# A transformer block with a routed feed-forward: turn 0 on a schedule of its own, and the last sequence routed and scattered in two halves

## The reference

```python
x = x + attention(layernorm(x))        # 16 heads of 32, softmax with a triangular mask
x = x + moe(layernorm(x))

def moe(x):                            # all 8192 tokens together
    scores = sigmoid(x @ router_w.T)
    topk_idx, topk_w = route(scores + e_bias)
    pos = rank of each (token, k) among those of its expert, in order of the tokens
    valid = pos < C                    # C = ceil(1.25 * 8192 / 32) = 320
    dest = expert * C + pos            # slots_token, slots_w filled at dest
    Y = (silu(Xp @ W_gate) * (Xp @ W_up)) @ W_down
    return scatter_add(Y * slots_w) + silu(x @ sg.T) * (x @ su.T) @ sd.T
```

## Time and profile before

| | |
|---|---|
| three runs | 2354.3, 2357.84, 2362.52 us; median 2357.84 |
| the profiled execution | 2342.3 us, its span 2340.6 us |
| busy over the span | PE 2171.2 us (93%), ACT 1636.1 (70%), DVE 1508.6 (64%), POOL 1032.8 (44%) |
| turn 0 | 18.2 (first projection) to 87.4 us |
| turn 1 | 87.4 to 182.8 us |
| turn 2; turn 3, like all up to 15 | 115.5 us; 114.1 us |
| turn 17 | 1871.9 (first output group) to 1938.3 (table load) |
| experts | from 1938.3 us to the end |

### The profile page before, as it was taken

How to read it: one execution, slowest core, us unless ns; L and a number is a source line. 1 busy time by engine, 2 the same in 40 slices (tenths; PEclk the granted TensorE clock), 3 DMA queues, 4 the chain that set the end, 5 groups by cost and what they waited for, 6 DMA issues and landing times. The chain is left out here.

```text
span 2340.6 us, 42190 instructions
## 1 busy us (share of the span) xinstructions
PE 2171.2 (93%) x13932; PEld 1139.9 (49%) x13932; DVE 1508.6 (64%) x5014; ACT 1636.1 (70%) x4025; POOL 1032.8 (44%) x1495
## 2 busy tenths in 40 slices
PE   7578999999999999999999999999998887999997
PEld 3234444444444444444444444444444444666664
DVE  4645666666767676666666667676667664767664
ACT  5688686867777878786868777777777524666664
POOL 3233134434344343434344343434342635777785
PEclk9799999999999999999999999999999997999999
DMA  7022222222222222222222222222212125999996
GB/s 235 16 53 61 56 74 58 72 58 78 62 71 65 68 71 63 75 68 65 64 64 64 64 64 64 64 64 64 64 46 82 29 99 166 248 247 248 244 249 130
DMA packets 158362, 222.40 MB, mean 95 GB/s; under 512 B 37824, under 2 KB 91168, under 8 KB 158144
## 3 DMA queue, kind: packets, MB, share of 16 engines
q1 hardware_dynamic: 129472, 177.58, 25.2%
q0 software_dynamic: 28672, 42.12, 8.8%
HBM read 112.65 MB, written 56.46 MB: 72 GB/s over the span
## 5 line engine op out<-in xcount | busy, mean ns | idle before, releaser
L745 ACT ACTIVATE junk<-junk,nmax 128x512 f32<-128x512 f32 (+3 forms) x1024 | 574.1, 570 | 160.1 <-DVE nmax L1046 157.9
L1046 DVE CUSTOM_DVE_ANT_0 junk<-scores,maskrow 128x512 f32<-128x512 f32 (+3 forms) x1024 | 464.9, 486 | 214.0 <-PE scores L591 185.8
L735 ACT ACTIVATE probs<-scores_T 128x512 f32<-128x512 f32 x640 | 376.4, 605 | 45.4 <-PE scores_T L608 45.3
L1211 POOL TENSOR_SCALAR_AFFINE_SELECT probs<-probs 128x256 f32<-128x256 f32 x512 | 194.5, 416 | 340.0 <-ACT probs L735 339.6
L1219 POOL DMA_INDIRECT slots_dram<-rec,idx x256 | 262.8, 1026 | 116.3 <-issue 80.7
L591 PE MATMUL scores<-stack_k,stack_q 96*128 96x512 f16 (+3 forms) x1024 | 249.0, 304 | 47.5 <-DVE nmax L1046 47.4
L608 PE MATMUL scores_T<-stack_q,stack_k 97*128 97x512 f16 (+3 forms) x1024 | 246.9, 303 | 31.4 <-ACT probs L735 27.5
L1204 POOL TENSOR_TENSOR split_q<-glu,split_q 128x512 f16<-128x512 f32 x64 | 76.9, 1202 | 390.6 <-ACT split_q L685 390.6
L745 ACT ACTIVATION_READ_ACCUMULATOR junk<-junk,nmax 128x1 f32 x1024 | 212.5, 207 | 0.0
L213 PE MATMUL dense<-xT_hi,wqkv_hi 128*128 128x512 f16 x512 | 197.0, 385 | 1.5 <-DVE xT_lo L1017 1.5
L214 PE MATMUL dense<-xT_lo,wqkv_hi 128*128 128x512 f16 x512 | 196.2, 383 | 0.0
(11 more groups left out here) (284 smaller groups left out, 5451.3 us busy)
## 6 DMA issues: line engine op xcount, KB each, us to landing
stack_q<-split_q SPq DMA_DIRECT2D x384, 64.0 KB, 2.0
stack_k<-split_k SPq DMA_DIRECT2D x384, 64.0 KB, 2.1
out<-xres SPq DMA_DIRECT2D x67, 256.0 KB, 3.1
x2n<-in_x SPq DMA_DIRECT2D x64, 256.0 KB, 3.7
xres<-in_x SPq DMA_DIRECT2D x64, 256.0 KB, 3.0
x2n_dram<-x2n SPq DMA_DIRECT2D x16, 1024.0 KB, 4.3
stack_q<-in_W_gate SPq DMA_DIRECT2D x16, 512.0 KB, 3.7
stack_q<-in_W_up SPq DMA_DIRECT2D x16, 512.0 KB, 5.3
```

The source lines that it names most:

```text
L735: act.activation(to, at, ACT.Exp, scale=SCALE / (QS * QS)).then_inc(exp_done, 1)
L745: last = act.activation(x, x, ACT.Exp, scale=-1.0, bias=c["nmax"][:, hg % 2, m:m + 1], accum_out=c["sums"][:, hg % 2, m:m + 1])
L1046: last = dve.tensor_tensor_reduce(out=c["junk"][:, JUNK_AT[f], at:at + cols], in0=ps["scores"][f % 2][:, at:at + cols], in1=c["maskrow"][: ...
L1211: last = pool.affine_select(out=blk, in_=blk, compare_op=ALU.is_ge, fill=0.0, base=0, pattern=[[0, 2], [1, P]], channel_multiplier=-1)
```

## The change

Turn 0 gets a plan of its own (`PLAN_0`): all ten score fills of group 0 (slots 50 to 68) and of group 1 (70 to 88) lie in turn 0, statistics at 42 to 54, and the side steps at earlier slots. ACT issues the k transfers of the first half. For sequence 0, ACT makes no `sums`; TensorE adds the probabilities with a product by ones after `values` (`probability_sums`), and `divide` on DVE takes the place of `spread_inverses`, `den_copy` and `normalise`. In turn 17 the router, the routing steps, `pos`, the places and the scatters are done for tiles 0 and 1, then for tiles 2 and 3, with five routing steps and four place steps a slot. `carried` gets a second copy. The function bodies of routing only get a range of tiles. In the middle turns the slots stay as they were.

```diff
+GROUPS_0 = ([(w, m, 4) for m in range(HG) for w in ("q", "k")] + [("v", t, 4) for t in range(TT)] + [("none", 0, 8)]
+            + [g for t in range(TT) for g in (("xT", t, 1), ("none", 0, 2))])
...
-GROUPS_17 = ([("out", t, 4) for t in range(TT)] + [("none", 0, 4)] + [("x2T", t, 1) for t in range(TT)] + [("router", 0, 4)]
-             + [(w, j, 4) for j in range(2) for w in ("gate", "up")] + [("pos", 1, 1)]
+GROUPS_17 = ([("out", t, 4) for t in range(TT)] + [("none", 0, 4)]
+             + [g for half in range(2) for g in (("x2T", 2 * half, 1), ("x2T", 2 * half + 1, 1), ("router", half, 2))]
+             + [g for half in range(2) for g in (("gate", half, 4), ("up", half, 4), ("pos", 1 + half, 1))]
              + [(w, j, 4) for j in range(2, IB) for w in ("gate", "up")] + [("down", t, 4) for t in range(TT)])
...
+S_AT_0 = {(0, 0): tuple(zip(range(50, 70, 2), range(FILLS))), (0, 1): tuple(zip(range(70, 90, 2), range(FILLS)))}
+S_AT_1 = {at: slots for at, slots in S_AT.items() if at != (1, 1)}
...
-PLAN_17 = Plan(GROUPS_17, 0, 3, ROUTE_STEPS, (), {})
+PLAN_0 = Plan(GROUPS_0, 100, 1, 0, (), {}, S_AT_0, (42, 46, 50, 54))
+PLAN_1 = Plan(GROUPS_1, 126, 1, 0, (), {}, S_AT_1)
+PLAN_17 = Plan(GROUPS_17, 0, 5, ROUTE_STEPS, (), {})
...
+def tiles_of(s):
+
+    if isinstance(s, int) and s >= BATCH - 1:
+        return range(2 * (s - BATCH + 1), 2 * (s - BATCH + 1) + 2)
+    return range(TT)
...
-SPLIT_SLOT = {slot: place for place, slot in zip(range(3, 8), (12, 22, 32, 42, 66))}
-
-BV_SPREAD, BV_PRODUCT, BV_ADDED = 70, 80, 84
-ROW_SLOT = {100 + 4 * hg: hg for hg in range(HG)}
+SPLIT_SLOT = {slot: place for place, slot in zip(range(3, 8), (8, 15, 22, 29, 92))}
+
+BV_SPREAD, BV_PRODUCT, BV_ADDED = 38, 49, 53
+ROW_SLOT = {slot: hg for hg, slot in enumerate((4, 12, 32, 35))}
+
+KEYS_SLOT = 41
...
             def stacks(i):
                 stack_ready(i, 0)
-                for name in ("q", "k"):
+                for name in ("q",) if in_first(i) else ("q", "k"):
                     for n in range(3):
-                        stack(name, n, 0)
+                        stack(sp, name, n, 0)
...
+            def first_keys():
+                act.wait_ge(qk_split, 2 * SHG)
+                for n in range(3):
+                    stack(act, "k", n, 0)
...
+            def probability_sums(s, hg):
+
+                pe.wait_ge(exp_done, (s * HG + hg + 1) * FILLS)
+                columns(ps["scores_T"][1], lambda kt, h: c["ones"][:, 0:HD]).then_inc(den_done, 1)
...
                     if attn and slot in PV_SLOT:
                         values(i - 1, 1 - par, PV_SLOT[slot])
+                        if in_first(i - 1):
+                            probability_sums(i - 1, PV_SLOT[slot])
...
+                if f == 0 and 0 < s * HG + hg <= HG:
+
+                    act.wait_ge(den_done, s * HG + hg)
...
+                        if of and not in_first(of[0]):
                             sums(*of, f)
...
+            def divide(s, hg):
+
+                n = s * HG + hg
+                by_block = c["denT"][:, :].rearrange("p (n r) -> p n r", r=HD)
+                dve.wait_ge(den_done, n + 1)
+                dve.transpose(c["denT"][:, :], ps["scores_T"][1][:, :]).then_inc(den_read, 1)
+                dve.wait_ge(den_read, n + 1)
+                link(dve.reciprocal(c["rden"][:, hg, :], by_block[:, :, 0]))
+                link(dve.tensor_copy(by_block, c["rden"][:, hg, :].unsqueeze(2).broadcast_to([P, SEQ // HD, HD])))
+                need(dve, aT_ready, n)
+                link(dve.transpose(c["att"][:, :], c["denT"][:, :]))
+                dve.wait_ge(o_done, n + 1)
+                dve.scalar_tensor_tensor(c["att"][:, :], ps["o"][:, :], AS, c["att"][:, :], ALU.mult, ALU.mult).then_inc(att_done, 1)
...
-                    if fin and slot >= plan.route_from:
-                        step = (slot - plan.route_from) * plan.route_pace
-                        for route in ROUTE[step:min(step + plan.route_pace, plan.route_now)]:
-                            route(i)
+                    for half, first in plan.route_from.items():
+                        if fin and slot >= first:
+                            step = (slot - first) * plan.route_pace
+                            for route in ROUTE[step:min(step + plan.route_pace, plan.route_now)]:
+                                route(i - 2 + half)
...
-                        if 0 <= step < len(DESTINATIONS):
-                            DESTINATIONS[step](s, bank)
+
+                        pace = 1 if attn else 4
+                        for destination in DESTINATIONS[max(step * pace, 0):max((step + 1) * pace, 0)]:
+                            destination(s, bank)
...
-            for n in range(TT * TOPK):
-                scatter(BATCH - 1, n)
+            for half in range(2):
+                for n in range(2 * TOPK):
+                    scatter(BATCH - 1 + half, n)
```

More of the change, by code:

```diff
@@ L99, in __init__ @@
         self.qlo = {ends[w, g] + 2: (w, g) for g in range(HG) for w in PROJ[0:2] if (w, g) in ends}
[L101 removed]
+        self.route_from = {half: ends.get(("router", half), 0) + 1 for half in range(2) if not half or ("router", half) in ends}
+        self.route_now, self.route_late = route_now, route_late
         self.last_h = ends.get(("up", IB - 1), 0) + 1
[L103 removed]
+        self.dest_from = {n: ends["pos", n] for n in range(3) if ("pos", n) in ends}
         self.scatter = {slot: (m, n) for m, slots in scatters.items() for n, slot in enumerate(slots)}
[L108 to L115 removed]
+        self.scores = {slot: (back, hg, f) for (back, hg), slots in (scores or S_AT).items() for slot, f in slots}
+        self.maxima = {slot + 1: at for slot, at in self.scores.items()}
+        self.maxima_T = {slot + 2: (back, hg) for slot, (back, hg, f) in self.scores.items() if f == FILLS - 1}
+        self.sums = {slot + 1: at for slot, at in self.maxima.items()}
+        self.shift = {slot + 2: at for slot, at in self.maxima_T.items()}
+        self.inverses = {slot + 5: at for slot, at in self.maxima_T.items()}
+        self.stat1 = {slot: t for t, slot in enumerate(stats)}
+        self.scale1 = {slot + 2: t for t, slot in enumerate(stats)}
+        self.ln1 = {slot + 10 - t: t for t, slot in enumerate(stats)}
 QUARTER = (0, 30, 60, 90)
@@ L388, in in_first, with score_group, stack @@
             return isinstance(i, int) and i == 0
-        def score_group(i, hg, proj, attn, f=FILLS):
-            if hg == 0 or (hg == 1 and f < S_EARLY):
-                return (i, hg) if proj else None
-            return (i - 1, hg) if attn else None
+        def score_group(i, back, hg, proj, attn):
+            if back:
+                return (i - 1, hg) if attn else None
+            return (i, hg) if proj else None
+        def stack(eng, name, n, half):
+            groups, part = slice(half * SHG, (half + 1) * SHG), {"q": (0, 1, 0), "k": (0, 0, 1)}[name][n]
+            for h in range(GH):
+                eng.dma_start(c["stack_" + name][n * HD:(n + 1) * HD, groups, h, :],
+                              c["split_" + name][part][h * HD:(h + 1) * HD, groups, :]).then_inc(stacked[half], 16)
         @block.sync
@@ L766, in turn @@
                         exp(i - 1, *EXP_SLOT[slot])
-                    if attn and slot in READ_SLOT:
+                    if attn and slot in READ_SLOT and not in_first(i - 1):
                         den_copy(i - 1, READ_SLOT[slot])
@@ L771, in turn @@
                     copies(par, slot, groups)
-                    if nxt and slot in LN1_SLOT:
-                        norm1(i + 1, LN1_SLOT[slot])
+                    if in_first(i) and slot == KEYS_SLOT:
+                        first_keys()
+                    if nxt and slot in plan.ln1:
+                        norm1(i + 1, plan.ln1[slot])
                     if fin and slot in plan.ln2:
@@ L965, in dest_equal @@
                 taken()
-                for t in range(TT):
+                for t in tiles_of(s):
                     last = dve.tensor_tensor(c["eq"][:, t, :, :], c["sc"][:, t, :].unsqueeze(1).broadcast_to([P, TOPK, E]),
@@ L1176, in _ @@
             chain["turn"] = chain["links"]
-            turns(dve, counted)
+            turns(dve, turn)
             for n, (name, _) in enumerate(WEIGHTS):
```

282 lines of the change are left out of this document (140 added, 142 removed).

## The result

The changed kernel takes **2349.24 us** in the median of 13 runs (2345.31 to 2353.09), the kernel before, run beside it, 2359.42 in 13 runs (2354.3 to 2362.52). The ratio is 0.9957, with an interval of 0.9949 to 0.9966: 10.2 us less, or 0.43%, with the whole interval outside the 0.3% that the prediction took as the least that can be told. The prediction had 2347.0 and a difference of 10.8.

What follows compares the result with a forecast made beforehand. VectorE was taken to bound turn 0's score half, ScalarE to lead two quarters of turn 1, a chain turn 17's end. 2342.3 - 8.6 - 2.2 + 0 = 2331.5, with 15.5 carried over 2347.0 us; range 2335 to 2358.

Steps and rivals of the forecast that it cites:

- Turn 0: Beginning of the kernel: earlier first score and less VectorE work in the score half start turn 1 8.6 us earlier.
- The issues: Turn 0: ScalarE issues 12 k transfers at 0.635 us each, bringing the first score at 56.0 instead of 57.75.
- the bound for a slow issue: Turn 0: at 1.28 us an issue, first score at 63.7 and turn 1 only 1.4 us earlier.
- Turn 1, new: Turn 1: sequence 0's sums leave ScalarE, probability_sums and divide come in; 93.2 us against 95.4, 2.2 us less.
- First: ... run at a low clock, as the 0.82 of this quarter shows: Turn 1, first quarter: half the fills and q0 at a low clock; 24.3 us instead of 26.4.
- Rival A: Turn 1 follows TensorE alone, without waits for exps and triangles: 12.9 us less instead of 2.2, 2336 us; chance 0.14.
- Turn 2: One of the middle turns, which TensorE fills and no edit touches; no change put in the sum.
- Turn 17: End of the block: first scatter 0.7 us earlier; table's load unchanged, between 0.7 us less and 2.5 more.
- rival C: VectorE's later end decides in turn 17 (+2.5 us) and turn 1 gains nothing: 2352 us; chance 0.10.
- Rival B: Turn 0: ScalarE's issues cost more or queue with SP's; gain 3.6 to 8 us, 2351 to 2354; chance 0.22.
- Rival D: Turn 1: TensorE's clock falls and the kernel gets slower, 7 us added, 2365 us; chance 0.05.
- The carry-over: Whole kernel: the three-run median's 15.5 us above the profiled execution, added to 2331.5 to give 2347.0 us.

Runs made afterwards that it cites:

- experiment 2: Changed kernel with turn 17 as before (last sequence routed in one piece, three steps a slot), so only the new beginning; 2330.73 us, ratio 0.9946.
- kernel 1: The kernel before, unchanged, run again for a second profile; median 2343.15 us, profiled execution 2339.65 us.
- experiment 6: Changed kernel with sequence 0's row sums kept on ScalarE, without probability_sums or divide; 2356.62 us, ratio 0.9977.
- experiment 10: kernel 7 with sgT's split and the spread put back late, so value_bias waits again; 2348.71 us, ratio 0.9959.
- experiment 11: kernel 7 with the four memsets back in turn 0's score half; 2356.86 us in a single run, no ratio drawn.
- Experiment 4: Changed kernel with the first half's k transfers issued by SP behind q, not by ScalarE; 2328.38 us, ratio 0.9936.
- experiment 3: Kernel before with only turn 17 changed (router, routing, places and scatters in halves), turns 0 and 1 as before; 2339.81 us, ratio 0.9987.
- the first group: The runs of kernel 1, experiment 2, experiment 3 and Experiment 4, on one chip; the kernel before had a median of 2343.15 us there.
- experiment 9: The kernel before, unchanged, profiled on a third chip; median 2358.76 us, profiled execution 2354.6 us.
- kernel 7: Changed kernel with SP issuing the k transfers and the last sequence routed in one piece, without halves; 2349.54 us, ratio 0.9935.
- kernel 5: The changed kernel again, unaltered, on a second chip; 2353.34 us, ratio 0.9961 to the kernel before.
- early_lo: kernel 7 with routing unbroken at seven steps a slot and VectorE's three first-expert weight splits ahead of its down-product additions; 2342.66 us, ratio 0.9931.

## Why the prediction was right, point by point

**The time and the sign** came out: a difference of 10.8 forecast, 10.2 measured. But one of its three terms, turn 1's 2.2 us, has a wrong reason, and that the sum comes within 0.6 us of the result is luck in part. In experiment 2 the beginning gains 12.4 us from median to median and 8.9 from profile to profile, and the sum has nothing for that difference; turn 2, ScalarE's issues and, where the stage of sequence 15 is long, the halves take something back.

**Turn 0: right in size.** The forecast had 8.6 us; kernel 2 beside kernel 1 has 9.35, and the first scores_T came at 78.2 for a forecast 78.8. The parts, from experiments 6, 10 and 11: the memsets, VectorE's share of the score half; value_bias's wait; and 2.8 to 3.3 us of sums that the forecast hadn't put here. They can't be added up, since they give back more together than the whole (13.0, 5.3 to 6.7 and 3.3 against 9.35): each brings a wait or a slow clock of its own. The statistics moved to earlier slots and the seven score fills taken over from turn 1 were not tried alone.

The issues were right too: 12 transfers on ScalarE in 8.00 us, 0.67 each where 0.635 was taken, and the first score at 55.95 for 56.0. By the bound for a slow issue, a first score at 63.7, its own steps leave turn 1 only 0.9 us earlier, not the 1.4 it names; nothing came to hang on that. What the forecast didn't see is that they need not have been moved at all. It named SP's 7.6 us of issuing "the bound", but that was read before value_bias was moved. The Trainium skill (DMA: Bandwidth & Descriptors, "Issuing engines are not separate DMA queues") says that a second issuing engine saves only the time of issuing. Experiment 4 agrees with it and goes further here, 1.3 us lost.

**Turn 1: the term was mis-reasoned.** "Turn 1, new" put 2.2 us on the sums' removal. The pair of profiles seems to say so, even more (95.43 to 92.51). But the kernel before took 92.16 and 92.47 us in its other two profiles, and the kernel with sums took 92.45. The kernels without the sums and with the whole beginning took 92.5 to 93.2. No gain shows. The step that failed is "First: ... run at a low clock, as the 0.82 of this quarter shows": it took one execution's clock for a property of the kernel and then took 2.1 us off that quarter, which is 22.9 us long against 23.1 in kernel 1. The second quarter did shrink by 1.5 (22.2, as forecast), and the last grew by 2.1 (28.1, forecast 27.2). TensorE's idle time in the last is 9.1 us before and after, so that growth is work, not a wait, and has the size of one group's probability sums. Over the whole turn TensorE has 4.5 us more to do than in kernel 1 (74.8 against 70.3) and 4.1 us less idle time. Rival A (12.9 us there) is out.

**Turn 2** was taken as untouched. It took 116.8 to 117.1 us instead of 115.5 in five of the seven profiles of kernels with the whole new beginning, and 115.7 and 115.8 in two; but also 116.9 in experiment 3, with the old one. Up to 1.6 us are not in the sum. It is the clock: TensorE's idle time in that turn is 4.9 to 5.0 us in every one of the profiles, and the mean granted clock is 0.985 to 0.988 where the turn is short and 0.974 to 0.977 where it is long. Whether the new beginning makes the low clock more likely can't be told from one profile of each kernel.

**Turn 17: right that the halves don't gain**, as far as the ratios tell, and right in the mechanism. Counted from sequence 15's last scores_T piece, kernels 2 and 4 (same chip, without and with halves): first scatter 46.43 and 46.46 (0.7 earlier forecast); VectorE's last split 64.6 and 71.7 (7.1 later; kernel 1 has 66.1, which makes it 5.6; 6.3 forecast); table's load 72.25 and 72.04. The changed kernel's second half on VectorE, first step, reciprocal, last step:

```profile
1904.55 0.19 DVE L884 TENSOR_SCALAR sig<-sig 128x64 f32<-128x64 f32 x1
1904.78 0.55 DVE L888 RECIPROCAL sig<-sig 128x64 f32<-128x64 f32 x1
...
1911.34 0.23 DVE L995 TENSOR_TENSOR wgt<-wgt,wsum 128x64 f32<-128x64 f32 x1
```

From its first step to the next work it takes 6.9 us, as the first half does, of which 0.6 is one step that isn't routing: 6.3 for a forecast of 6.6. A 128x64 step takes 0.23, as in the earlier trace rows. The figure of 58 cycles drawn from the Trainium skill (VectorE: DVE Perf Modes, "The TRN2 errata") gave 0.13 and does not hold for these steps. The same section also states (elements + 151)/0.96 GHz for a tensor_tensor in fp32, an estimated 0.224 us at 64 elements, and with that the trace agrees.

Where the stage of sequence 15 is long, the halves cost: 77.6, 80.1 and 77.9 with them, 73.7 to 76.0 without in five profiles (experiment 9's among them). Against kernel 7's 76.0 on the same chip, kernels 5 and 6 pay 4.1 and 1.9. That is rival C's price (+2.5), about, and the two of the first group (72.0) don't pay it. The traces say which end decides. In all five profiles with the halves the load comes 0.3 us behind VectorE's last split. In the seven with routing as before it comes 5.0 us behind the start of the last scatter. In the first group the two ends happen to lie level (72.0 and 72.25), as the forecast had them; elsewhere VectorE's is the later one.

**Rival B** (ScalarE's issues cost more) has its mechanism in small: a wait of 0.91 us, and 1.3 us of cost. **Rival D** didn't come: the first quarter's clock is 0.95. Its mirror image did: it is the kernel *before*, and kernel 3 with the same beginning, that let the clock fall in some executions, behind value_bias's wait or in the first quarter. That its median therefore lies further above its best profile fits, but isn't shown. The beginning alone gains 8.9 us from profile to profile, and 12.4 from median to median.

**The carry-over** of 15.5 us from profile to median came out by luck, for a reason that the forecast didn't have. The profile was of an execution with the short stage of sequence 15, and the runs, to judge by their times, were like experiment 9's.

## What to carry to other kernels

Before a term is built on a low clock in one stretch of one execution, look whether the same code runs at it every time: here 3.3 us and 3.0 us were such. Work moved from one engine to another is paid for on the other: here 25.8 us less on ScalarE and 4.5 more on TensorE made nothing, since TensorE was the one with little to spare. A wait ahead of TensorE costs itself and at times the clock behind it (3.0 us cost 6), so it can be worth more than its length to remove. When several causes of one late start are changed together, try each back alone: one may cost (the issues on ScalarE), one may bring nothing that can be measured (the halves), and the next bound is then visible (VectorE's tail, which moving three splits into an idle time took off the end).

## What was not expected of the hardware

The same kernel showed 84.5 us in one stage on one chip and 95.8 on another, at equal counts, the granted clock 0.94 and 0.89; its medians were 2343.2, 2358.8 and 2362.9 us on three chips (2359.4 in the first runs). The ratios are steadier: 0.9957 and 0.9961 for the changed kernel in two groups, 0.9936 and 0.9935 for kernels 4 and 7.

A wait of 3.0 us in front of the same eight products left them at 0.44 us each, start to start, in three profiles and at 0.87 in one (0.69 after one of 3.8); the granted clock over them was 1.00 in the three, 0.55 and 0.68 in the other two.

Scatters on POOL take 0.97 us mostly, and 1.97 now and then. POOL in early_lo:

```profile
1926.54 1.04 POOL L1292 DMA_INDIRECT slots_dram<-rec,idx  x1 [0.31 <-issue]
1927.88 1.97 POOL L1292 DMA_INDIRECT slots_dram<-rec,idx  x1 [0.30 <-issue]
1930.16 1.97 POOL L1292 DMA_INDIRECT slots_dram<-rec,idx  x1 [0.30 <-issue]
1932.43 0.97 POOL L1292 DMA_INDIRECT slots_dram<-rec,idx  x1 [0.30 <-issue]
```

The two of 1.97 us lie beside VectorE's splits (1927.78 to 1931.28). In every one of the eight profiles whose last scatters overlap these splits, one or two take 1.96 to 1.99 us; in the six without such an overlap, none of the turn's 16 takes over 1.5. Not every scatter in the overlap takes so long: in kernel 7 the one at 1939.55, just before the long one, takes 0.97. That VectorE's splits cause it was not tried by itself. In early_lo this is 2.0 us of the landing that now decides.
